# A two-layer graph kernel on one core: the features' bias and relu leave GpSimd, b2 is added ahead of the strips, and the row gathers are cut into other lots

## The chip, the cores and the metric

One core of one Trainium2 chip. The metric is the device time of one execution in microseconds (us). The engines are called PE (TensorE, the matmuls), DVE (VectorE), ACT (ScalarE), POOL (GpSimd) and SP (SyncE, which here only issues transfers).

## The reference

```
h = relu(layernorm(x));  x = x + L0(h, adj)
h = relu(layernorm(x));  x = x + L1(h, adj)

L0:  tanh(concat[h, t] @ W1 + b1) @ W2 + b2
     + adj @ (h @ B.T) - rowsum(adj) * (h @ B.T)
L1:  feats = h @ W                      (8 heads of 8)
     scores = leaky_relu(a_self[i] + a_neigh[j]) - 1e10 * (1 - adj[i, j])
     relu(softmax(scores) @ feats + bias)
```

x is 8192 x 64 and adj is 8192 x 8192, both float32, so adj is 256 MB. adj holds values from 0 to 1, not zeros and ones, so the term of -1e10 leaves for each row only the neighbour with the largest adj. The second layer's output for row i is therefore relu(feats[best[i]] + bias), with best[i] the column of the largest value of row i. The kernel checks at its end that this shortcut held and has a general path behind a branch, which does not run here.

## The kernel before, in words

**Strips and chunks.** The 8192 rows are 16 strips of 512 rows (S = 16), a strip is four tiles of 128 rows (TB = 4), 64 tiles in all. Of each strip adj arrives transposed in 8 chunks of 2 MB. SP loads them into a ring of four slots (`load`); a slot is loaded again when PE (`pe_chunk`) and DVE (`hi_done`) have both used it.

**PE**, for each strip: `sums` and `products` of the 8 chunks (row sums and adj @ h). Between them stand the small steps of the strip before: `turn_maxima(s-1)`, which waits for DVE's `runmax_done`; `turn_sums(s-1)`, `turn_h1(s-1)`, `features(s-1)`; and at the end `mlp_hidden(s)`.

**DVE**, for each strip: `fold_chunk` takes the running maximum over the chunks (two operations of 128x2048 each), `fold_maxima` folds it down to `runmax` (L623, L625, L628). Between chunks 3 and 4 stand `search_classes(s-1)`, which finds for each row the class of columns that holds the maximum (`cls_row`, L646), and `residual(s-1)` with the second layernorm; `search_candidates(s-1)` after chunk 6 gives `best`.

**ACT** copies PE's results out of PSUM (`finish_strip`), with the tanh, the square root and the copy of `feats` (L541).

**POOL** is one queue in program order. For each strip: `add_b2(s)` (L393: x_tq + b2, 128x256), `store_agg(s-1)` (L400: feats + bias; L404: maximum with 0; L406: a store of 128 KB to `agg_dram`, and a wait until it has landed), `fetch_candidates(s)` (L413: four indirect transfers). From strip 11 on it also gathers `agg_dram[best]` (L420: one indirect transfer for a tile of 128 rows). Strips 0 to 14 are gathered in five lots, by the table `WINDOWS = (known, s0, s1)`: once agg is stored for strips below `known`, strips s0 to s1 are gathered. The rows of which `best` lies in a strip that was not yet stored are mended at the end: up to 8 for each partition (`SLOTS`), gathered again by L453 and added to the output by L463. The last strip's four tiles are gathered with these.

**The head.** Strip 0 runs while DVE and ACT normalise x (`centre`, `normalise`: L602 is the last operation of each eighth, `pro_norm`). PE's `products` of chunk c waits for `pro_norm` c+1. `constants()` (L567 to L577) stands on DVE before the last chunk's fold; PE's first `mlp_hidden` waits for it. `x_tq` is loaded by SP behind the chunks of strip 0, and POOL's first `add_b2` waits for that load.

**The tail.** After PE has finished strip 15, DVE works out `best` for the last strip, `add_x1` (L764) adds the residual to the gathered rows, SP stores them, and POOL issues what is left of its queue.

Of the kernel before, what the change touches and what calls it, by code (L numbers as in the profile page):

```python
# [23 lines left out]
ALU = mybir.AluOpType  # L24
# [12 lines left out]
CB = 8  # L37
# [11 lines left out]
SPAN = 8192  # L49
WINDOWS = ((11, 0, 3), (12, 3, 6), (13, 6, 9), (14, 9, 12), (15, 12, 15))  # L50
EARLY = 12 * TB
LATE = 15 * TB


def build(nc, x, adj, adj_t, w1, w1_t, b1, t_in, w2, b2, b_t, w_gat, w_gat_t, att_self, att_neigh, bias, out):
    with ExitStack() as ctx:
        def sb(name, shape, dt=F32):
            return ctx.enter_context(nc.sbuf_tensor(name, shape, dt))
# [4 lines left out]
        def sem(name):  # L63
            return ctx.enter_context(nc.semaphore(name))
# [60 lines left out]
        good = sb("good", [P, 6])  # L125
        agg = sb("agg", [P, TB * D])
        agg_last = sb("agg_last", [P, TB, D])
        is_late = sb("is_late", [P, LATE])
# [64 lines left out]
        zero_stored = sem("zero_stored")  # L193
        agg_chain = sem("agg_chain")
        agg_stored = sem("agg_stored")
# [27 lines left out]
        dve_past = sem("dve_past")  # L223
        pe_past = sem("pe_past")

        gen_turned = sem("gen_turned")
# [111 lines left out]
        def _(pool):  # L338
# [51 lines left out]

            def add_b2(s):
                x1 = x_tq[:, bass.ds(s * TB, TB), :]
                pool.tensor_tensor(x1, x1, b2_row[:, :].unsqueeze(1).to_broadcast([P, TB, D]),  # L393
                                   ALU.add).then_inc(x_b2_done, 1)

            def store_agg(s):

                pool.wait_ge(feat_done, s + 1)
                a = feats_v[:, bass.ds(s * TB, TB), 0:D]
                pool.tensor_tensor(agg[:, :].rearrange("q (k d) -> q k d", d=D), a,  # L400
                                   bias_row[:, :].unsqueeze(1).to_broadcast([P, TB, D]), ALU.add).then_inc(agg_chain, 1)
                pool.wait_ge(agg_chain, s * 2 + 1)
                pool.sem_inc(pool_past, 1)
                pool.tensor_scalar(agg[:, :], agg[:, :], 0.0, None, ALU.max).then_inc(agg_chain, 1)  # L404
                pool.wait_ge(agg_chain, s * 2 + 2)
                pool.dma_start(agg_by_q[:, bass.ds(s, 1), :].rearrange("q a f -> q (a f)"), agg[:, :]).then_inc(agg_stored, 16)  # L406
                pool.wait_ge(agg_stored, s * 16 + 16)

# [15 lines left out]

            def round_(s):
                add_b2(s)
                store_agg(s - 1)
                fetch_candidates(s)

            add_b2(0)  # L430
            fetch_candidates(0)
            n0 = WINDOWS[0][0]
            with pool.Fori(1, n0) as s:
                round_(s)
            for w, (known, s0, s1) in enumerate(WINDOWS):
                add_b2(known)
                if w:
                    pool.wait_ge(got[w - 1], 16 * TB * (WINDOWS[w - 1][2] - WINDOWS[w - 1][1]))
                store_agg(known - 1)
                pool.wait_ge(best_done, s1)  # L440
                if known < S - 1:
                    gather(w, s0 * TB, s0 * TB + TB)
                    fetch_candidates(known)
                    gather(w, s0 * TB + TB, s1 * TB)
                else:
                    gather(w, s0 * TB, s1 * TB)
                    fetch_candidates(known)

# [29 lines left out]
        def _(act):  # L478
# [42 lines left out]

            def finish_strip(s, last=False):

# [22 lines left out]
            act.wait_ge(dve_const, 4)  # L546
            with act.Fori(0, S - 1) as s:
                finish_strip(s)
# [12 lines left out]
        def _(dve):  # L561
# [104 lines left out]
            def residual(s):  # L666
# [8 lines left out]
                dve.wait_ge(chain, c0 + 2)  # L675
                dve.wait_ge(x_b2_done, s + 1)
                dve.tensor_tensor(x1, x1, tmp[:, :, :], ALU.add).then_inc(x1_done, 1)
# [17 lines left out]

            def strip(s):

                dve.wait_ge(runmax_done, s)
                for c in range(NC):
                    fold_chunk(s, c)  # L700
                    if c == 3:
                        search_classes(s - 1)
                        residual(s - 1)
                    if c == 4:
                        scale_h1(s - 1)
                    if c == 6:
# [15 lines left out]
            fold_maxima(0)  # L722
            with dve.Fori(1, S) as s:
                strip(s)
            search_classes(S - 1)
            residual(S - 1)
# [337 lines left out]
```

## Time and profile before

| what | value |
|---|---|
| median of 3 runs | 844.42 us (842.97 to 845.2) |
| the profiled execution | 846.39 us, its span 844.7 us |
| PE, DVE, POOL, ACT busy | 767.9, 732.3, 316.0, 130.0 us |
| PE's granted clock, mean | 0.96 of full |
| transfers | 282.80 MB, mean 335 GB/s over the span |

Busy time is the time in which an engine executes; the span runs from the first to the last instruction. A granted clock of 1.00 is 2.4 GHz, and 0.50 is 1.2 GHz. A DVE or POOL duration includes the time that the instruction waited for its operands' path into SBUF, so an operation of one shape can show different durations.

### The profile page before, as it was taken

The numbers are of one execution on the slowest core, as the hardware profiler recorded it, in microseconds if no ns is written. First come the engines' busy times: TensorE is split into PE (matmuls) and PEld (weight loads), VectorE is DVE, ScalarE is ACT, GpSimd is POOL, SyncE is SP. The second block draws the span as 40 slices with busy tenths as digits, with TensorE's granted clock in tenths as the row PEclk, the third lists the DMA queues.
The fourth block names the chain that finished last, engine by engine and source line by source line (L and its number), as shares of the span: only waits on it lengthen the run. The fifth ranks groups of instructions, "written<-read, shape, count | busy, mean of one in ns | idle before, by whom it ended". The sixth has DMA issues, their size and how long they took to land.

```text
span 844.7 us, 13444 instructions
## 1 busy us (share of the span) xinstructions
PE 767.9 (91%) x5222; PEld 275.6 (33%) x5222; DVE 732.3 (87%) x963; ACT 130.0 (15%) x212; POOL 316.0 (37%) x247
## 2 busy tenths in 40 slices
PE   4998999999999999999999999999999999999100
PEld 1333333333434343333334343333334343433100
DVE  4899998999998989989898999989898999999420
ACT  2344011020202011110202020111102020111100
POOL 7000312212131313111131313131586868778775
PEclk9998999999999999999999999999999999999655
DMA  8997898999898998989898998989998999983152
GB/s 331 419 401 287 316 380 331 396 368 386 324 388 343 370 379 334 380 355 399 337 383 328 388 379 332 377 336 383 371 385 348 390 359 374 397 335 137 26 124 21
DMA packets 30190, 282.80 MB, mean 335 GB/s; under 512 B 6176, under 2 KB 10640, under 8 KB 13664
## 3 DMA queue, kind: packets, MB, share of 16 engines
q1 hardware_dynamic: 23168, 275.00, 81.1%
q0 software_dynamic: 7008, 7.63, 3.8%
q8 instruction: 7, 0.11, 0.1%
q14 instruction: 7, 0.06, 0.0%
HBM read 277.37 MB, written 5.24 MB: 335 GB/s over the span
## 4 chain that ended last, share of the span: by engine, by line
PE 67%; POOL 18%; DMA 9%; issue 4%; DVE 1%; ACT 0%; SPq 0%; POOLq 0%; DVEq 0%; ACTq 0%
PE acc L869 39%; PE row_sums L877 20%; POOL gathered L420 10%; DMA ring<-in_adj_t 4%; POOL cand L413 3%; DMA gathered<-agg_dram,best 2%; DMA agg_dram<-agg 2%; PE ps_hid L884 1%; POOL out L463 1%; POOL agg L404 1%; POOL agg L400 1%; PE ps_feat L926 1%; PE ps_xb L905 1%; PE ps_acc L898 1%; POOL max_hi L453 1%
## 5 line engine op out<-in xcount | busy, mean ns | idle before, releaser
L869 PE MATMUL acc<-ring,x_pb 128*64 128x512 f32 x2048 | 449.7, 596 | 0.0
L877 PE MATMUL row_sums<-ring,ones_cols 128*32 128x512 f32 x2048 | 235.0, 604 | 13.0 <-DMA ring<-in_adj_t 13.0
L616 DVE TENSOR_TENSOR max_lo<-max_lo,ring 128x2048 f32<-128x2048 f32 x96 | 220.6, 2298 | 28.2 <-DMA ring<-in_adj_t 27.5
L869 PEld LDWEIGHTS acc<-ring,x_pb 128*64 128x64 f32 x2048 | 144.2, 137 | 283.9 <-issue 280.6
L617 DVE TENSOR_TENSOR max_hi<-max_hi,ring 128x2048 f32<-128x2048 f32 x96 | 219.2, 2283 | 0.0
L413 POOL DMA_INDIRECT cand<-in_adj,cls_row x64 | 83.7, 1308 | 225.8 <-DVE cls_row L646 210.0
L420 POOL DMA_INDIRECT gathered<-agg_dram,best x64 | 110.2, 1722 | 40.3 <-DMA agg_dram<-agg 22.3
L877 PEld LDWEIGHTS row_sums<-ring,ones_cols 128*32 128x32 f32 x2048 | 61.7, 111 | 158.8 <-issue 156.5
L400 POOL TENSOR_TENSOR agg<-feats,bias_row 128x256 f32<-128x256 f32 x15 | 24.7, 1648 | 192.8 <-ACT feats L541 187.9
L393 POOL TENSOR_TENSOR x_tq<-x_tq,b_row 128x256 f32 (+1 forms) x16 | 26.1, 1634 | 42.6 <-DMA x_tq<-in_x 42.2
L541 ACT COPY feats<-ps_feat 128x320 f32 (+1 forms) x16 | 6.8, 427 | 218.5 <-PE ps_feat L926 216.5
L623 DVE TENSOR_TENSOR max_lo<-max_lo,max_hi 128x2048 f32<-128x2048 f32 x16 | 36.7, 2293 | 2.0
L611 DVE TENSOR_TENSOR max_lo<-ring 128x2048 f32<-128x2048 f32 x16 | 36.7, 2292 | 2.0
L613 DVE TENSOR_TENSOR max_hi<-ring 128x2048 f32<-128x2048 f32 x16 | 38.2, 2386 | 0.0
L534 ACT ACTIVATE stat<-stat,eps 128x4 f32<-128x4 f32 x16 | 4.8, 298 | 184.8 <-DVE stat L688 184.8
L404 POOL TENSOR_SCALAR agg<-agg 128x256 f32<-128x256 f32 x15 | 26.3, 1754 | 3.0 <-POOL agg L400 3.0
L625 DVE TENSOR_TENSOR max_lo<-max_lo 128x1024 f32<-128x1024 f32 x16 | 24.6, 1535 | 0.5
L655 DVE MAX8 top_cand<-cand 128x8 f32<-128x64 f32 x64 | 9.6, 212 | 14.5 <-DMA cand<-in_adj,cls_row 14.5
L990 PE MATMUL ps_hid<-ones,good 128*1 128x1 f32 x2 | 0.2, 164 | 23.9 <-DVE good L792 23.9
L884 PE MATMUL ps_hid<-h_strip,w_sb 128*128 128x256 f32 x64 | 19.0, 421 | 2.9 <-ACT h_strip L519 2.9
L534 ACT ACT_TABLE_LOAD x16 | 20.5, 1283 | 0.3
L513 ACT ACT_TABLE_LOAD x16 | 20.5, 1283 | 0.3
(130 smaller groups left out, 481.8 us busy)
## 6 DMA issues: line engine op xcount, KB each, us to landing
ring<-in_adj_t SPq DMA_DIRECT2D x128, 2048.0 KB, 8.7
agg_dram<-agg POOLq DMA_DIRECT2D x20, 128.0 KB, 6.9
x_tq<-in_x SPq DMA_DIRECT2D x1, 2048.0 KB, 14.0
x_pb<-in_x SPq DMA_DIRECT2D x1, 1536.0 KB, 14.6
out<-gathered SPq DMA_DIRECT2D x1, 1536.0 KB
cand<-in_adj,cls_row POOLq DMA_INDIRECT x64
gathered<-agg_dram,best POOLq DMA_INDIRECT x64, 6.2
x_pb<-in_x SPq DMA_DIRECT2D x1, 512.0 KB, 4.6
```

The costliest lines, as they stand in the source:

```text
L400: pool.tensor_tensor(agg[:, :].rearrange("q (k d) -> q k d", d=D), a, bias_row[:, :].unsqueeze(1).to_broadcast([P, TB, D]), ALU.add).then_ ...
L404: pool.tensor_scalar(agg[:, :], agg[:, :], 0.0, None, ALU.max).then_inc(agg_chain, 1)
L413: pool.indirect_dma_start(out=cand[:, k, :], out_offset=None, in_=classes, in_offset=bass.IndirectOffsetOnAxis(ap=cls_row[:, k:k + 1], axi ...
L420: pool.indirect_dma_start(out=gathered[:, t, :], out_offset=None, in_=agg_dram, in_offset=bass.IndirectOffsetOnAxis(ap=best[:, t:t + 1], a ...
L611: dve.tensor_tensor(max_lo[:, :], lo, hi, ALU.max).then_inc(hi_done, 1)
L613: dve.tensor_tensor(max_hi[:, :], lo, hi, ALU.max).then_inc(hi_done, 1)
L616: dve.tensor_tensor(max_lo[:, :], max_lo[:, :], lo, ALU.max).then_inc(lo_done, 1)
L617: dve.tensor_tensor(max_hi[:, :], max_hi[:, :], hi, ALU.max).then_inc(hi_done, 1)
L623: dve.tensor_tensor(max_lo[:, :], max_lo[:, :], max_hi[:, :], ALU.max).then_inc(fold, 1)
L869: last = pe.matmul(acc[0][at:at + D, :], x_pb[:, c * CB + b, :], slot(c)[:, b * W:(b + 1) * W], start=(c == 0 and b < 2), stop=(c == NC - ...
L877: last = pe.matmul(row_sums[at:at + QUAD, :], ones_cols[:, :], slot(c)[:, b * W:(b + 1) * W], start=(c == 0 and b < 4), stop=(c == NC - 1 ...
L884: last = pe.matmul(ps_hid[:, k * (W // 2):(k + 1) * (W // 2)], w1_sb[:, k * HID:(k + 1) * HID], h_strip[:, :], start=True, stop=True)
```

## The change

POOL's two arithmetic operations for each strip leave it. DVE adds the bias (`add_bias(s-2)`, behind the first fold of strip s, into a new buffer `agg_pre`), ACT takes the relu (`rectify(s-1)`, behind the tanh in `finish_strip`), and POOL only issues the store, whose landing is now awaited before the gathers and no longer right behind the store. The 16 additions of b2, one for each strip, become four of 128x1024 ahead of strip 0's candidates; `residual` waits for all four. The lots change from 12, 12, 12, 12, 12 tiles to 8, 16, 16, 16 and 4; the candidates are fetched ahead of the gathers, but for the last strip behind them. `EARLY`, the rows that the first large `add_x1` takes, goes from 48 to 56 tiles.

```diff
-WINDOWS = ((11, 0, 3), (12, 3, 6), (13, 6, 9), (14, 9, 12), (15, 12, 15))
-EARLY = 12 * TB
+WINDOWS = ((11, 0, 2), (12, 2, 6), (13, 6, 10), (14, 10, 14), (15, 14, 15))
+EARLY = 14 * TB
...
-            def add_b2(s):
-                x1 = x_tq[:, bass.ds(s * TB, TB), :]
-                pool.tensor_tensor(x1, x1, b2_row[:, :].unsqueeze(1).to_broadcast([P, TB, D]),
+            def add_b2(g):
+                x1 = x_tq[:, g * CB * 2:(g + 1) * CB * 2, :]
+                pool.tensor_tensor(x1, x1, b2_row[:, :].unsqueeze(1).to_broadcast([P, CB * 2, D]),
                                    ALU.add).then_inc(x_b2_done, 1)
 
             def store_agg(s):
 
-                pool.wait_ge(feat_done, s + 1)
-                a = feats_v[:, bass.ds(s * TB, TB), 0:D]
-                pool.tensor_tensor(agg[:, :].rearrange("q (k d) -> q k d", d=D), a,
-                                   bias_row[:, :].unsqueeze(1).to_broadcast([P, TB, D]), ALU.add).then_inc(agg_chain, 1)
-                pool.wait_ge(agg_chain, s * 2 + 1)
-                pool.sem_inc(pool_past, 1)
-                pool.tensor_scalar(agg[:, :], agg[:, :], 0.0, None, ALU.max).then_inc(agg_chain, 1)
-                pool.wait_ge(agg_chain, s * 2 + 2)
+                pool.wait_ge(agg_ready, s + 1)
                 pool.dma_start(agg_by_q[:, bass.ds(s, 1), :].rearrange("q a f -> q (a f)"), agg[:, :]).then_inc(agg_stored, 16)
-                pool.wait_ge(agg_stored, s * 16 + 16)
...
-            add_b2(0)
+            for g in range(NB // (2 * CB)):
+                add_b2(g)
             fetch_candidates(0)
...
             for w, (known, s0, s1) in enumerate(WINDOWS):
-                add_b2(known)
                 if w:
                     pool.wait_ge(got[w - 1], 16 * TB * (WINDOWS[w - 1][2] - WINDOWS[w - 1][1]))
                 store_agg(known - 1)
+                if known < S - 1:
+                    fetch_candidates(known)
+                pool.wait_ge(agg_stored, 16 * known)
                 pool.wait_ge(best_done, s1)
...
+                gather(w, s0 * TB, s1 * TB)
+            fetch_candidates(S - 1)
...
+            def rectify(s, first):
+                if first:
+                    act.wait_ge(zero_stored, 16 * (S - WINDOWS[0][0]))
+                else:
+                    act.wait_ge(agg_stored, s * 16)
+                act.sem_inc(act_past, 1)
+                act.wait_ge(agg_pre_ready, s + 1)
+                act.activation(agg[:, :], agg_pre[:, :], ACT.Relu).then_inc(agg_ready, 1)
...
                 tanh(s)
+                if behind:
+                    rectify(s - 1, behind == 1)
                 act.wait_ge(acc_turned, s + 1)
...
-                dve.wait_ge(x_b2_done, s + 1)
+                dve.wait_ge(x_b2_done, NB // (2 * CB))
...
+            def add_bias(s):
+
+                dve.wait_ge(feat_done, s + 1)
+                dve.tensor_tensor(agg_pre[:, :].rearrange("q (k d) -> q k d", d=D), feats_v[:, bass.ds(s * TB, TB), 0:D],
+                                  bias_row[:, :].unsqueeze(1).to_broadcast([P, TB, D]), ALU.add).then_inc(agg_pre_ready, 1)
...
                 for c in range(NC):
                     fold_chunk(s, c)
+                    if c == 0 and not first:
+                        add_bias(s - 2)
...
+            add_bias(S - 2)
             search_classes(S - 1)
```

POOL's queue before, from the last zero store through the loop's body over strips 1 to 10 (line numbers are those of each kernel; ISA and REGISTER_ALU rows are waits and their bookkeeping):

```order
L384 DMA agg_dram<-agg 128x256 x5
L393 TENSOR_TENSOR x_tq<-x_tq,b_row 128x256
L413 DMA cand<-in_adj,cls_row 128x64 x4
L433 UNCONDITIONAL_BRANCH
L433 ISA
L393 TENSOR_TENSOR x_tq<-x_tq,b_row 128x256
L400 ISA
L400 TENSOR_TENSOR agg<-feats,bias_row 128x256
L402 ISA
L404 TENSOR_SCALAR agg<-agg 128x256
```

The same place now:

```order
L387 DMA agg_dram<-agg 128x256 x5
L396 TENSOR_TENSOR x_tq<-x_tq,b_row 128x1024 x4
L408 DMA cand<-in_adj,cls_row 128x64 x4
L424 UNCONDITIONAL_BRANCH
L402 ISA
L402 DMA agg_dram<-agg 128x256
L405 REGISTER_ALU
L408 DMA cand<-in_adj,cls_row 128x64 x4
```

Four additions, each of four times the width, now stand ahead of the first candidates, and the loop's body holds no arithmetic.

POOL's queue before, from the gathers of the lot `known = 14` to the first mending gathers:

```order
L406 DMA agg_dram<-agg 128x256
L420 DMA gathered<-agg_dram,best 128x64 x4
L413 DMA cand<-in_adj,cls_row 128x64 x4
L420 DMA gathered<-agg_dram,best 128x64 x8
L393 TENSOR_TENSOR x_tq<-x_tq,b_row 128x256
L400 TENSOR_TENSOR agg<-feats,bias_row 128x256
L404 TENSOR_SCALAR agg<-agg 128x256
L406 DMA agg_dram<-agg 128x256
L420 DMA gathered<-agg_dram,best 128x64 x12
L413 DMA cand<-in_adj,cls_row 128x64 x4
L453 DMA max_hi<-agg_dram,late_from 128x64 x8
```

The same place now:

```order
L402 DMA agg_dram<-agg 128x256
L408 DMA cand<-in_adj,cls_row 128x64 x4
L415 DMA gathered<-agg_dram,best 128x64 x16
L402 DMA agg_dram<-agg 128x256
L415 DMA gathered<-agg_dram,best 128x64 x4
L408 DMA cand<-in_adj,cls_row 128x64 x4
L442 DMA max_hi<-agg_dram,late_from 128x64 x8
```

Sixteen gathers stand ahead of the last store and four behind it, where twelve and twelve stood (four of the first twelve ahead of the candidates), and three arithmetic operations between them are gone.

DVE's program now, at the start of the body of strips 2 to 15:

```order
L613 TENSOR_TENSOR max_lo<-ring 128x2048
L700 REGISTER_ALU
L701 ISA
L701 TENSOR_TENSOR agg_pre<-feats,bias_row 128x256
L615 TENSOR_TENSOR max_hi<-ring 128x2048
```

The addition of 128x256 in the middle is the new one; the two folds around it are as before.

## Rows read from the trace of the kernel before

**Rows 1.** The page: busy time, granted clock by slices, the chain that ended last.

```profile
PE 767.9 (91%) x5222; PEld 275.6 (33%) x5222; DVE 732.3 (87%) x963; ACT 130.0 (15%) x212; POOL 316.0 (37%) x247
...
PEclk9998999999999999999999999999999999999655
...
PE 67%; POOL 18%; DMA 9%; issue 4%; DVE 1%; ACT 0%; SPq 0%; POOLq 0%; DVEq 0%; ACTq 0%
```

**Rows 2.** Windows: length, busy time of PE, PEld, DVE, ACT, POOL; clock, DMA share, GB/s.

```profile
262.80:309.71 46.91, 46.91 (x324) 16.78 (x323) 43.72 (x56) 6.61 (x12) 10.36 (x8) 1.00 0.90 363
731.08:778.05 46.97, 46.97 (x324) 16.82 (x324) 43.85 (x56) 6.63 (x12) 35.80 (x20) 1.00 0.71 280
```

**Rows 3.** The waits: engine, line, what for: us in all, times, longest.

```profile
DVE max_lo L616 <- DMA ring<-in_adj_t: 27.5, 30, 2.4
```

**Rows 4.** Timeline of the head: start, us, instruction [idle before <-releaser].

```profile
59.56 0.74 POOL L393 TENSOR_TENSOR x_tq<-x_tq,b_row 128x256 f32<-128x256 f32 x1 [42.24 <-DMA x_tq<-in_x]
...
60.92 0.69 DVE L602 SCALAR_TENSOR_TENSOR x_pb<-x_pb,pstat 128x512 f32<-128x512 f32 x1
...
66.65 0.20 DVE L577 COPY fold_rows<-pstat 128x64 f32<-128x64 f32 x1
...
74.86 0.69 DVE L628 TENSOR_TENSOR runmax<-max_lo 128x512 f32<-128x512 f32 x1
...
72.01 2.05 PE L884 MATMUL ps_hid<-h_strip,w_sb 128*128 128x256 f32 x4 [2.92 <-ACT h_strip L519]
...
79.45 0.66 PE L912 MATMUL ps_turn<-ident,runmax 128*128 128x128 f32 x4
```

**Rows 5.** Timeline: operations of POOL and DVE that meet, in strips 1 and 2.

```profile
100.37 2.98 DVE L616 TENSOR_TENSOR max_lo<-max_lo,ring 128x2048 f32<-128x2048 f32 x1 [0.22 <-DMA ring<-in_adj_t]
...
100.44 0.74 POOL L393 TENSOR_TENSOR x_tq<-x_tq,b_row 128x256 f32 x1
...
165.18 2.29 DVE L623 TENSOR_TENSOR max_lo<-max_lo,max_hi 128x2048 f32<-128x2048 f32 x1
165.90 2.16 POOL L400 TENSOR_TENSOR agg<-feats,bias_row 128x256 f32<-128x256 f32 x1 [16.35 <-ACT feats L541]
167.51 1.64 DVE L625 TENSOR_TENSOR max_lo<-max_lo 128x1024 f32<-128x1024 f32 x1
```

**Rows 6.** Timeline: the same of DVE, L625 with no POOL operation beside it, and L613.

```profile
73.60 1.23 DVE L625 TENSOR_TENSOR max_lo<-max_lo 128x1024 f32<-128x1024 f32 x1
...
733.43 2.82 DVE L613 TENSOR_TENSOR max_hi<-ring 128x2048 f32<-128x2048 f32 x1
```

**Rows 7.** Timeline of POOL: its smallest operation that reads and writes SBUF.

```profile
3.56 0.19 POOL L352 TENSOR_SCALAR_AFFINE_SELECT head_mask<-head_mask 64x8 f32<-64x8 f32 x1
```

**Rows 8.** Timeline of POOL from strip 15's candidates to the end.

```profile
750.74 0.95 POOL L413 DMA_INDIRECT cand<-in_adj,cls_row  x1 [0.30 <-issue]
...
774.36 2.12 POOL L420 DMA_INDIRECT gathered<-agg_dram,best  x1 [0.30 <-issue]
776.50 1.00 POOL L393 TENSOR_TENSOR x_tq<-x_tq,b_row 128x256 f32<-128x256 f32 x1
778.08 0.73 POOL L400 TENSOR_TENSOR agg<-feats,bias_row 128x256 f32<-128x256 f32 x1 [0.58 <-DMA gathered<-agg_dram,best]
...
780.16 0.64 POOL L406 DMA_DIRECT2D agg_dram<-agg  x1 [0.30 <-POOL agg L404]
782.51 1.03 POOL L420 DMA_INDIRECT gathered<-agg_dram,best  x1 [1.71 <-DMA agg_dram<-agg]
...
791.62 3.89 POOL L420 DMA_INDIRECT gathered<-agg_dram,best  x1 [0.30 <-issue]
...
804.63 0.96 POOL L413 DMA_INDIRECT cand<-in_adj,cls_row  x1 [0.30 <-issue]
```

**Rows 9.** Timeline of DVE at the end: the last fold and the first large addition.

```profile
776.95 1.10 DVE L628 TENSOR_TENSOR runmax<-max_lo 128x512 f32<-128x512 f32 x1
...
791.35 3.34 DVE L764 TENSOR_TENSOR gathered<-gathered,x_tq 128x3072 f32<-128x3072 f32 x1
```

More of the change, by code:

```diff
@@ L126, in build @@
         agg = sb("agg", [P, TB * D])
+        agg_pre = sb("agg_pre", [P, TB * D])
         agg_last = sb("agg_last", [P, TB, D])
@@ L193, in build @@
         zero_stored = sem("zero_stored")
-        agg_chain = sem("agg_chain")
+        agg_pre_ready = sem("agg_pre_ready")
+        agg_ready = sem("agg_ready")
         agg_stored = sem("agg_stored")
@@ L224, in build @@
         pe_past = sem("pe_past")
+        act_past = sem("act_past")
         gen_turned = sem("gen_turned")
@@ L423, in gather @@
                     ).then_inc(got[w], 16)
[L425 to L428, printed above, removed]
-            add_b2(0)
+            for g in range(NB // (2 * CB)):
+                add_b2(g)
             fetch_candidates(0)
@@ L433, in _ @@
             with pool.Fori(1, n0) as s:
-                round_(s)
+                store_agg(s - 1)
+                fetch_candidates(s)
             for w, (known, s0, s1) in enumerate(WINDOWS):
-                add_b2(known)
                 if w:
@@ L439, in _ @@
                 store_agg(known - 1)
+                if known < S - 1:
+                    fetch_candidates(known)
+                pool.wait_ge(agg_stored, 16 * known)
                 pool.wait_ge(best_done, s1)
[L441 to L447, printed above, removed]
+                gather(w, s0 * TB, s1 * TB)
+            fetch_candidates(S - 1)
             pool.wait_ge(agg_last_stored, 16)
@@ L520, in strip_h, with finish_strip @@
                              h_by_k[:, 2 * k:2 * k + 2, bass.ds(s * P, P)]).then_inc(strip_h_done, 1)
-            def finish_strip(s, last=False):
+            def rectify(s, first):
[6 more added lines that the diff above has]
+                act.activation(agg[:, :], agg_pre[:, :], ACT.Relu).then_inc(agg_ready, 1)
+            def finish_strip(s, last=False, behind=2):
                 act.wait_ge(acc_full, s + 1)
@@ L546, in _ @@
             act.wait_ge(dve_const, 4)
-            with act.Fori(0, S - 1) as s:
+            finish_strip(0, behind=0)
+            finish_strip(1, behind=1)
+            with act.Fori(2, S - 1) as s:
                 finish_strip(s)
@@ L694, in scale_h1, with strip @@
                 dve.tensor_tensor(h1[:, :, :], cen[:, :, :], wide(rstd[:, :], TB), ALU.mult).then_inc(h1_done, 1)
-            def strip(s):
+            def add_bias(s):
+                dve.wait_ge(feat_done, s + 1)
+                dve.tensor_tensor(agg_pre[:, :].rearrange("q (k d) -> q k d", d=D), feats_v[:, bass.ds(s * TB, TB), 0:D],
+                                  bias_row[:, :].unsqueeze(1).to_broadcast([P, TB, D]), ALU.add).then_inc(agg_pre_ready, 1)
+            def strip(s, first=False):
                 dve.wait_ge(runmax_done, s)
@@ L722, in _ @@
             fold_maxima(0)
-            with dve.Fori(1, S) as s:
+            strip(1, first=True)
+            with dve.Fori(2, S) as s:
                 strip(s)
+            add_bias(S - 2)
             search_classes(S - 1)
```

## The prediction

> **What bounds the kernel now.** I read the page first: PE is busy 91% of the span, DVE 87%, POOL only 37%, but the chain that ended last holds 67% of PE and 18% of POOL, and the clock's last slices are low [rows 1]. So there are two stages: strips in which PE is the chain, and a tail in which something on POOL is. The windows say it sharply: in a middle strip PE is busy 46.91 of 46.91 us at a clock of 1.00, DVE 43.72, and the strip in which POOL works 35.80 us takes the same 46.97 [rows 2]. Nothing that takes work off POOL or DVE there can shorten a strip. DVE has spare time: it waited 27.5 us for chunks in 30 waits over the run [rows 3].
>
> The tail is POOL's queue. It issues the candidates of strip 14 from 750.74, and from 774.36 on one thing follows the other with no gap but for landings, to the last candidate of strip 15 at 804.63; the mending gathers, their scatters and the last store stand behind that and take the rest of the 844.7 us [rows 8]. DVE's last fold ends already at 778.05 [rows 9].
>
> The head is a third stage. POOL's first addition of b2 starts at 59.56, when x_tq has landed. DVE ends runmax of strip 0 at 75.55 (74.86 + 0.69) and PE uses it at 79.45, behind its own work [rows 4]: 3.9 us of slack, of which I leave 0.15 to the semaphore, so 3.75.
>
> **The change part by part.**
>
> *Bias on DVE, relu on ACT: nothing.* One addition of 128x256 costs DVE 0.4 us a strip, at a place that is followed by the waits for chunks 2 and 3; those 27.5 us over 15 strips are 1.8 a strip and cover it [rows 3]. DVE also gets back what POOL's operations took from it, below. If that cover were gone, the cost would be 14 x 0.4 = 5.6 us. ACT is busy 6.6 us in a strip of 47 [rows 2]; the copy of acc_tq is queued behind the relu, and DVE's residual waits for that copy, but `add_bias` needs only fold 0 of the strip (2.3 us), and PE's small steps come later than that.
>
> *The 15 relus, 15 bias additions and 15 of 16 additions of b2 that leave POOL's strips.* They ran under PE. They are worth something only in the tail: the last three.
>
> *Four additions of 128x1024 in the head.* This is the expensive part. What a POOL operation does to DVE is to be seen in the two places where they meet. At 100.44 POOL adds 256 columns in 0.74 us, and the fold of 2048 columns that started 0.07 before takes 2.98 instead of 2.29: 0.69 lost. At 165.90 POOL has to wait (2.16 instead of 0.74), gets its turn when the fold L623 ends at 167.47, and L625 behind it takes 1.64 [rows 5] instead of 1.23; L613 at 733.43 takes 2.82 instead of 2.29 [rows 6]. So they exclude each other, POOL gets its turn at the next boundary of DVE's two-input operations, and 256 columns cost DVE 0.41, 0.53 or 0.69 us. The head had one such addition, and it was over before L602 began [rows 4].
>
> The width now is four times. How long is 1024 columns? No row shows one. The smallest POOL operation takes 0.19 [rows 7]; if that is the fixed part, 0.55 us is for 256 columns and 1024 take 0.19 + 4 x 0.55 = 2.39. Then the first runs from 59.56 to 61.95 and holds DVE's L602 (start 60.92) by 1.0. The other three are queued, each gets its turn behind one DVE operation (L602, L616, L617), and each holds the next one by four times 0.41 to 0.69, that is 1.6 to 2.8; I take 2.0. Together runmax of strip 0 is 1.0 + 3 x 2.0 = 7.0 us later. PE absorbs 3.75 of it, so PE is late by 7.0 - 3.75 = 3.2 us. `mlp_hidden(0)` waits for fold_rows too, which moves from 66.85 to 73.9, past its old start of 72.01 by 1.9 [rows 4]; that is less than 3.2 and lies in it. PE has no gap later in which to win it back, so it stays to the end: **+3.2**. Bounds: if only half of an add's cost scales with its width, the first holds nothing and the queued ones 1.6 each, 4.8, so +1.1; if everything scales, 4 x 0.74 = 2.96 for the first (1.6 held) and 2.8 for each of the others, 10.0, so +6.3.
>
> The Trainium skill's GPSIMD Engine Reference (3.1, Elementwise) gives 4.5 us for such an addition of 2048 columns; between that and 0.74 here, 1024 would be 2.35 by estimate, close to 2.39. The skill's SBUF page ("SBUF — State Buffer", SBUF: two separate sides) says that whichever starts first keeps the shared port pair "for the whole instruction"; taken at its word with 2.35 for all four, DVE would be late by about 8.1 and PE by 4.3. The rows at 100.44 agree with the rule and those of the queued operation show less. No row here shows a wide one.
>
> DVE itself is late by 7.0 and PE by 3.2 going into strip 1. The slots of the ring that DVE frees late (chunks 6 and 7 of strip 0) carry chunks 2 and 3 of strip 1, which PE needs only after some 12 us of other work. DVE then gains on PE by its spare 1 to 3 us a strip, so I cost this at nothing.
>
> *The lots and the tail.* POOL is free at strip 14's candidates in both kernels. From 750.74 to 776.48 it issues 12 items (four candidates, eight gathers), at 2.1 us each, because under DVE's folds an issue waits for their boundaries [rows 8]. Now 8 of 16 gathers are left at 776.8: one under DVE's last fold (2.2), seven at 1.26 (the pace behind 782.51), so to 787.5. The landing of the last takes 1.6 (776.48 to 778.08), the store's 2.35 (780.16 to 782.51) [rows 8]: four gathers start at 791.5. The large `add_x1` starts then on DVE: it took 3.34 us for 3072 columns and stretched one gather to 3.89 [rows 8, 9]; 3584 columns make 3.9 and about 4.4. So the four end at 799.7, and four candidates at 1.26 each end at 804.7, against 805.6. That is 0.9 won; if one more gather fits before 776.48, since the candidates no longer stand behind four gathers, it is 2.1. I take **-1.5**. Bounds: 0 when a landing takes 1 us more, and -4.5 if `add_x1` falls into the wait for the store instead of on a gather. It is this little since the number of issues in the chain is the same (28); the lot of four only moves eight gathers ahead of the store, and what is truly gone are the three POOL operations, 776.50 to 780.16 less a landing of 1.6.
>
> Sum: +3.2 - 1.5 = +1.7 us. The profiled execution took 846.39 (span 844.7), so it would be 848.1; the median of the runs is 0.2% lower, 844.42, and becomes **846.1**.
>
> **The rivals.**
>
> *The head is hidden, the tail gains (faster).* If the additions hold DVE by less than 3.75 us altogether, PE never sees them. That decides it: under 0.9 for each of four. For it: 0.41 at 256 columns may be mostly a handover that doesn't grow. Against: 0.69 of 0.74 was lost at 100.44. Then the time is 844.4 less 1.5 to 4.5: 840 to 843, say 842.
>
> *The additions hold DVE for their whole length at four times 0.74 (slower).* PE late by 6.3, 844.4 + 6.3 - 1.5 = 849.2. For it: the unqueued row. Against: both queued rows show less. It decides for "slower" as soon as DVE loses over 7.8 us.
>
> *The lots of 16 don't fit under a strip.* Twenty issues at 2.1 are 42 us, with the landings and the store 46 of 46.9. If POOL falls behind, candidates come late, and each us is added at strip 15: some 3 us, 849. DVE's small operations, where an issue takes 1.26, speak against it.
>
> *It doesn't do what it says:* it would have to keep POOL's arithmetic in the strips or leave the mending list too short; the order shows that the first is gone, and the second would let the general path run, whose operations this trace lacks.
>
> **How the numbers follow.** The forecast has 0.48, with its own range 843.5 to 848; the hidden head 0.28; the full hold 0.16; the lots that don't fit 0.08. What a measurement here can tell from no change is 0.3%, 2.5 us, so 841.9 to 846.9 is "same". The forecast's case lies in it for four fifths, else above; the hidden head is faster in three of four. Faster 0.21, same 0.45, slower 0.34. The range leaves out 1 in 10 on each side: 841.0 to 849.5.
>
> **What would show it.** POOL's four additions from 59.56, 2.4 us or more each; DVE's L602, L616, L617 around 61 to 73 stretched by 2; runmax of strip 0 at about 82.5 and PE's first turn of it at 82.7 for 79.45; strips of 46.9 after that; POOL's last candidate at 804.7 plus 3.2. Wrong would be: a PE that turns the maxima at 79.5, a tail shorter by more than 4 us, or a strip that is no longer full of PE.

## The result and the profile after

The changed kernel takes 853.87 us (median of 5 runs, 853.54 to 855.06) against 844.42 before (842.97 to 848.17): a ratio of 1.011, 95% interval 1.0083 to 1.0136. The forecast was 846.1 in a range that ended at 849.5. The profiled execution took 853.87, its span 852.1.

The page after, to be held against [rows 1]: busy time, granted clock, the chain that ended last.

```profile
PE 766.7 (90%) x5222; PEld 275.4 (32%) x5222; DVE 732.2 (86%) x978; ACT 135.9 (16%) x227; POOL 254.5 (30%) x205
...
PEclk9998999999999999999999999999999999999655
...
PE 64%; POOL 16%; DVE 8%; issue 6%; DMA 4%; POOLq 0%; ACT 0%; SPq 0%; DVEq 0%
```

POOL lost 61.5 us of work, ACT has 5.9 us more (the relu), the others have as much as before, and yet the span is 7.4 us longer. What is new is DVE with 8% of the chain. The windows say that it isn't in the middle; the same stretches as in [rows 2]:

```profile
262.80:309.71 46.91, 46.91 (x324) 16.73 (x322) 43.21 (x57) 6.93 (x12) 5.55 (x5) 1.00 0.91 364
731.08:778.05 46.97, 46.97 (x326) 16.73 (x322) 42.45 (x57) 6.94 (x12) 35.67 (x20) 1.00 0.82 316
```

PE is as full as before at the same clock. From PE's turn of h in strip 1 to its last group of products it is 656.38 us, before 656.41. So the loss is ahead of that and behind it.

**The head after**, timeline (start, us, instruction, idle time before and its releaser), for [rows 4]:

```profile
60.30 13.85 POOL L396 TENSOR_TENSOR x_tq<-x_tq,b_row 128x1024 f32<-128x1024 f32 x4 [42.98 <-DMA x_tq<-in_x]
...
60.59 2.61 DVE L604 SCALAR_TENSOR_TENSOR x_pb<-x_pb,pstat 128x512 f32<-128x512 f32 x1
63.12 4.45 DVE L618 TENSOR_TENSOR max_lo<-max_lo,ring 128x2048 f32<-128x2048 f32 x1
67.50 4.45 DVE L619 TENSOR_TENSOR max_hi<-max_hi,ring 128x2048 f32<-128x2048 f32 x1
71.87 2.43 DVE L569 TENSOR_SCALAR att_diag<-head_mask,att_col 64x8 f32<-64x8 f32 x2
...
82.88 0.69 DVE L630 TENSOR_TENSOR runmax<-max_lo 128x512 f32<-128x512 f32 x1
...
63.34 3.65 PE L881 MATMUL acc<-ring,x_pb 128*64 128x512 f32 x16 [1.31 <-DVE x_pb L604]
74.36 0.40 PE L989 MATMUL ps_feat<-att_diag,w_gat_t_sb 64*64 64x16 f32 x4 [4.51 <-DVE hid_bias L571]
76.16 2.05 PE L896 MATMUL ps_hid<-h_strip,w_sb 128*128 128x256 f32 x4 [1.40 <-ACT h_strip L508]
83.62 0.66 PE L924 MATMUL ps_turn<-ident,runmax 128*128 128x128 f32 x4 [1.21 <-DVE runmax L630]
108.21 0.41 PE L931 MATMUL ps_turn<-ident,h 128*128 128x128 f32 x2 [0.86 <-DVE h L696]
```

Each of the four additions holds one stretch of DVE: L604 by 1.9 us (2.61 for 0.69), two folds by 2.16 each (4.45 for 2.29), att_diag by 2.1 (2.43 for 0.35). runmax of strip 0 ends at 83.57 for 75.55, 8.0 later, and PE turns it at 83.62 for 79.45, 4.2 later. Then comes a wait that the forecast hadn't: PE waits 0.86 us for h of strip 1, at 108.21.

**The tail after**, for [rows 8, 9]:

```profile
661.46 0.97 POOL L408 DMA_INDIRECT cand<-in_adj,cls_row  x1 [14.54 <-DVE cls_row L648]
...
701.33 3.05 POOL L415 DMA_INDIRECT gathered<-agg_dram,best  x1 [0.30 <-issue]
710.01 0.59 POOL L402 DMA_DIRECT2D agg_dram<-agg  x1 [5.62 <-DMA gathered<-agg_dram,best]
...
760.34 0.59 POOL L402 DMA_DIRECT2D agg_dram<-agg  x1 [5.82 <-DMA gathered<-agg_dram,best]
761.23 2.48 POOL L408 DMA_INDIRECT cand<-in_adj,cls_row  x1 [0.30 <-issue]
...
797.32 0.59 POOL L402 DMA_DIRECT2D agg_dram<-agg  x1 [1.78 <-DMA gathered<-agg_dram,best]
799.61 0.97 POOL L415 DMA_INDIRECT gathered<-agg_dram,best  x1 [1.69 <-DMA agg_dram<-agg]
...
806.22 4.49 POOL L408 DMA_INDIRECT cand<-in_adj,cls_row  x1 [0.31 <-issue]
...
812.27 0.95 POOL L408 DMA_INDIRECT cand<-in_adj,cls_row  x1 [0.30 <-issue]
...
785.41 0.41 ACT L518 ACTIVATE agg<-agg_pre 128x256 f32<-128x256 f32 x1
797.69 0.38 ACT L530 COPY acc_tq<-ps_acc 128x260 f32<-128x260 f32 x1 [11.88 <-remote]
...
806.00 3.88 DVE L776 TENSOR_TENSOR gathered<-gathered,x_tq 128x3584 f32<-128x3584 f32 x1
```

POOL starts strip 12's candidates on time (it had waited 14.54 us). Its 20 issues end at 704.38, 42.9 us later. Then it stands 5.62 us for the landing of the lot: 48.6 us from those candidates to the store at 710.01, a strip having 46.9. The next such stretch takes 50.3. In the table below, strip 14's first candidate is so 5.4 us later against PE than before. And ACT stands still for 11.88 us ahead of its copy of acc_tq, which pushes DVE's large add_x1 to 806.00. There it falls on a candidate, whose issue takes 4.49 us; before, it fell on a gather, which took 3.89 [rows 8].

To compare kernels I count from marks of the same trace. In the head: PE's turn of the eighth part of x (61.37 before, 60.97 after) as zero. In the tail: the start of PE's last group of products (759.53 and 764.59) as zero. All in us; the names are explained above.

| | runmax turned | h of strip 1 turned | strip 14's first candidate | large add_x1 | last candidate ends |
|---|---|---|---|---|---|
| before | 18.1 | 41.8 | -8.8 | 31.8 | 46.1 |
| after | 22.7 | 47.2 | -3.4 | 41.4 | 48.6 |
| e5 after again | 22.9 | 47.5 | -3.3 | 41.4 | 48.6 |
| e1 head only | 22.8 | 47.5 | -9.0 | 31.7 | 44.6 |
| e7 16 x 256 in head | 20.1 | 46.0 | -3.1 | 41.4 | 48.6 |
| e2 b2 spread | 17.1 | 40.7 | -2.7 | 32.5 | 46.1 |
| e8 before, b2 spread | 15.3 | 39.0 | -8.8 | 31.7 | 46.0 |
| e4 bias and relu only | 16.9 | 40.6 | -9.1 | 31.7 | 47.2 |
| e3 old lots | 22.7 | 47.3 | -9.0 | 31.8 | 47.3 |
| e6 b2 spread, lots 12 12 16 16 4 | 17.3 | 40.9 | -6.2 | 39.6 | 46.9 |
| e9 b2 spread, covered landings | 16.9 | 40.6 | -9.0 | 31.8 | 44.1 |
| e10 after, covered landings | 22.8 | 47.4 | -9.0 | 31.8 | 44.1 |

### The profile page after: what moved, and what is told of

Read it like the earlier page. It is cut to its first block, busy times and chain, and to the rows that moved or that the text cites. A ratio compares the mean times of both kernels' runs of the same rounds, so it can differ in the third digit from the quotient of the medians.

```text
span 852.1 us, 13399 instructions
## 1 busy us (share of the span) xinstructions
PE 766.7 (90%) x5222; PEld 275.4 (32%) x5222; DVE 732.2 (86%) x978; ACT 135.9 (16%) x227; POOL 254.5 (30%) x205
## 4 chain that ended last, share of the span: by engine, by line
PE 64%; POOL 16%; DVE 8%; issue 6%; DMA 4%; POOLq 0%; ACT 0%; SPq 0%; DVEq 0%
PE acc L881 38%; PE row_sums L889 19%; POOL gathered L415 10%; DMA ring<-in_adj_t 4%; POOL cand L408 3%; DVE max_hi L619 3%; DVE max_lo L618 2%; PE ps_hid L896 1%; POOL out L452 1%; PE ps_feat L938 1%; PE ps_xb L917 1%; PE ps_acc L910 1%; POOL max_hi L442 1%; PE ps_turn L924 1%; PE ps_acc L915 1%
## 5 line engine op out<-in xcount | busy, mean ns | idle before, releaser
L408 POOL DMA_INDIRECT cand<-in_adj,cls_row x64 | 90.7, 1418 | 218.2 <-DVE cls_row L648 202.7
L415 POOL DMA_INDIRECT gathered<-agg_dram,best x64 | 105.7, 1651 | 20.9 <-issue 18.6
L402 POOL DMA_DIRECT2D agg_dram<-agg x15 | 8.9, 592 | 299.8 <-ACT agg L518 286.6
L625 DVE TENSOR_TENSOR max_lo<-max_lo,max_hi 128x2048 f32<-128x2048 f32 x16 | 36.7, 2292 | 2.0
L613 DVE TENSOR_TENSOR max_lo<-ring 128x2048 f32<-128x2048 f32 x16 | 36.7, 2291 | 1.9
L396 POOL TENSOR_TENSOR x_tq<-x_tq,b_row 128x1024 f32<-128x1024 f32 x4 | 13.8, 3490 | 43.0 <-DMA x_tq<-in_x 43.0
L537 ACT ACTIVATE h_t<-ps_turn 128x256 f32<-128x256 f32 x15 | 5.8, 384 | 90.6 <-PE ps_turn L931 90.6
L627 DVE TENSOR_TENSOR max_lo<-max_lo 128x1024 f32<-128x1024 f32 x16 | 19.6, 1225 | 0.5
L530 ACT COPY acc_tq<-ps_acc 128x260 f32<-128x260 f32 x16 | 6.0, 375 | 77.7 <-PE ps_xb L917 65.8
L776 DVE TENSOR_TENSOR gathered<-gathered,x_tq 128x256 f32<-128x256 f32 (+1 forms) x3 | 4.7, 1575 | 15.8 <-DMA gathered<-agg_dram,best 15.8
## 6 DMA issues: line engine op xcount, KB each, us to landing
agg_dram<-agg POOLq DMA_DIRECT2D x20, 128.0 KB, 20.1
```

Source lines behind the costliest of these rows:

```text
L408: pool.indirect_dma_start(out=cand[:, k, :], out_offset=None, in_=classes, in_offset=bass.IndirectOffsetOnAxis(ap=cls_row[:, k:k + 1], axi ...
L415: pool.indirect_dma_start(out=gathered[:, t, :], out_offset=None, in_=agg_dram, in_offset=bass.IndirectOffsetOnAxis(ap=best[:, t:t + 1], a ...
L613: dve.tensor_tensor(max_lo[:, :], lo, hi, ALU.max).then_inc(hi_done, 1)
L625: dve.tensor_tensor(max_lo[:, :], max_lo[:, :], max_hi[:, :], ALU.max).then_inc(fold, 1)
```

## The experiments

**e1, the four additions alone.** The kernel before, with its 16 additions replaced by the four in the head.

```diff
...
-            add_b2(0)
+            for g in range(NB // (2 * CB)):
+                add_b2(g)
...
-                dve.wait_ge(x_b2_done, s + 1)
+                dve.wait_ge(x_b2_done, NB // (2 * CB))
```

> The kernel before with one part of the change: the four additions of b2 of 128x1024 in the head, and none in the strips. Theory (the head stalls PE for good, and the lots cost the rest): PE's first matmul of strip 1 moves from 82.2 to about 87.3 us and stays 5 us late to the end; POOL's tail loses its addition of 1.0 us ahead of the last store, so +4 to +5 us against the kernel before, a ratio of 1.005 to 1.006. Rival (the loss of the changed kernel comes from the bias on DVE and the relu on ACT, and PE wins the head back): within 1.5 us of the kernel before.

Measured: 850.5 us, ratio 1.0069 (1.005 to 1.0089). The table shows the head of the changed kernel, so the additions alone make it. Its timeline shows who is held:

```profile
59.70 13.20 POOL L393 TENSOR_TENSOR x_tq<-x_tq,b_row 128x1024 f32<-128x1024 f32 x4 [42.38 <-DMA x_tq<-in_x]
...
59.45 2.29 DVE L615 TENSOR_TENSOR max_lo<-max_lo,ring 128x2048 f32<-128x2048 f32 x1
61.65 4.46 DVE L616 TENSOR_TENSOR max_hi<-max_hi,ring 128x2048 f32<-128x2048 f32 x1
66.03 4.60 DVE L566 TENSOR_SCALAR att_diag<-head_mask,att_col 64x8 f32<-64x8 f32 x2
...
70.73 2.20 DVE L571 TENSOR_TENSOR hid_bias<-hid_bias 128x1 f32<-128x1 f32 x1
```

In this execution DVE was further on: L604's counterpart had ended at 59.53, so POOL's first addition, released at 59.70, was queued behind a fold that had begun. All four additions then hold something: the next fold by 2.17, the two small operations of 64x8 by 2.1 each (4.60 for 0.35) and one of 128x1 by 2.04. Whatever DVE does next pays. PE waits for h of strip 1 (0.94 us) and once more for h of strip 2 (1.06 us), so here DVE's lateness outlives strip 1.

**e2, b2 in pieces.** The changed kernel with b2 as eight additions of 128x512, one in the head and one in each of strips 1 to 7.

```diff
-                x1 = x_tq[:, g * CB * 2:(g + 1) * CB * 2, :]
+                x1 = x_tq[:, bass.ds(g * CB, CB), :]
...
+            with pool.Fori(1, NB // CB) as s:
+                add_b2(s)
+                store_agg(s - 1)
+                fetch_candidates(s)
...
```

> The changed kernel with the additions of b2 taken out of the head: eight of 128x512, one ahead of strip 0's candidates and one in each of strips 1 to 7. Theory: the head's stall of PE is gone, PE's first products of strip 1 at about 82.5 us, and the rest of the loss (POOL late at strip 14's candidates) stays: +2.5 us against the kernel before (ratio 1.003), 7 us less at the last pieces than the changed kernel is over before. Rival (the loss is in bias, relu or lots alone): +8 us or more stays, ratio 1.009.

Measured: 844.65 us, ratio 0.9996 (0.9983 to 1.0009). The whole loss is gone, more than expected (a ratio of 1.003), for the tail came out better too. POOL is as late as in the changed kernel (-2.7), but ACT doesn't stand still:

```profile
59.92 1.27 POOL L396 TENSOR_TENSOR x_tq<-x_tq,b_row 128x512 f32<-128x512 f32 x1 [42.56 <-DMA x_tq<-in_x]
...
781.49 0.38 ACT L533 COPY acc_tq<-ps_acc 128x260 f32<-128x260 f32 x1 [2.14 <-PE ps_xb L920]
...
790.64 3.89 DVE L779 TENSOR_TENSOR gathered<-gathered,x_tq 128x3584 f32<-128x3584 f32 x1 [0.69 <-DMA gathered<-agg_dram,best]
793.09 2.29 POOL L415 DMA_INDIRECT gathered<-agg_dram,best  x1 [1.69 <-DMA agg_dram<-agg]
```

add_x1 lies mostly in the wait for the store, and the gather behind it takes 2.29 where a candidate took 4.49. Of the profiles here it is the only one in which add_x1 meets that wait; elsewhere it lengthens an issue to 3.3 to 4.5 us. So the 46.1 of e2 is in part a lucky meeting: its last store starts 32.7 us behind the start of the last products, as late as in the changed kernel.

**e3, the lots of before.** The changed kernel with the old table.

```diff
-WINDOWS = ((11, 0, 2), (12, 2, 6), (13, 6, 10), (14, 10, 14), (15, 14, 15))
-EARLY = 14 * TB
+WINDOWS = ((11, 0, 3), (12, 3, 6), (13, 6, 9), (14, 9, 12), (15, 12, 15))
+EARLY = 12 * TB
```

> The changed kernel with the lots of the kernel before (five of 12 tiles), in the new order (candidates ahead of the gathers). Theory: POOL is not behind at strip 14's candidates any more (first of them within 1 us of DVE's cls_row), but the chain behind them has 4+12+12+4 = 32 issues for 28, so 4 x 1.26 = 5 us more of issuing against 5.4 us less of lateness: the same time as the changed kernel within 2.5 us, +8 to +11 us against before. Rival (the large last but one lot itself is the loss, not the lateness): 4 us or more faster than the changed kernel.

Measured: 851.26 us, ratio 1.0093 (1.0074 to 1.0112). With 16 issues a strip POOL is on time (-9.0), and the last candidate comes at 47.3. So the large lots are a loss of 1.3 us against the old ones in this program, although the old ones leave four more issues for the end, and the head remains.

**e4, bias and relu alone** moved in the kernel before (the `add_bias` and `rectify` of the diff).

```diff
...
-                pool.wait_ge(feat_done, s + 1)
...
+                pool.wait_ge(agg_ready, s + 1)
...
```

> The kernel before with one part of the change: the bias added on DVE and the relu taken on ACT, while b2, lots and order of the gathers stay. Theory: PE's strips stay at 46.9 us; POOL loses two operations and their gaps ahead of the last store (1.9 us), so -1 to -2.5 us against before (ratio 0.997 to 0.999). Rival (the moved work costs: the copy of acc_tq waits behind the relu, DVE is late with each strip): slower than before by 2 us or more, with PE late by a few tenths in each strip.

Measured: 844.71 us, ratio 1.0004 (0.9987 to 1.0022). None of the 1 to 2.5 us that were expected, and the timeline of its tail says why:

```profile
772.40 2.17 POOL L396 TENSOR_TENSOR x_tq<-x_tq,b_row 128x256 f32<-128x256 f32 x1
779.48 0.60 POOL L402 DMA_DIRECT2D agg_dram<-agg  x1 [4.91 <-ACT agg L525]
```

The store waits 4.91 us for the relu, which stands behind ACT's tanh. POOL's two operations went, a wait for ACT took their place.

**e5, the changed kernel again.**

> The changed kernel once more, unaltered. In its first profile ACT stood still for 11.9 us ahead of the last copy of acc_tq, and the large addition on DVE then started at 806.0 and held one of POOL's candidate issues (4.49 us). Theory (the standstill belongs to this program and costs the 2.5 us that the tail is longer than in e2_spread_b2): it is there again, the last candidate ends 48.6 us behind the start of PE's last products, and the time is 9 us over before. Rival (a matter of that one execution): ACT waits 2 us there, the last candidate ends about 46 us behind that start, and the median of the runs has another part that is not explained yet.

Measured: 852.68 us, ratio 1.0095 (1.007 to 1.012). ACT's standstill is there again (11.81 us, the copy at 796.31), so it isn't an accident of one execution.

**e6, the lots 12, 12, 16, 16, 4** on e2.

```diff
-WINDOWS = ((11, 0, 2), (12, 2, 6), (13, 6, 10), (14, 10, 14), (15, 14, 15))
+WINDOWS = ((11, 0, 3), (12, 3, 6), (13, 6, 10), (14, 10, 14), (15, 14, 15))
```

> e2_spread_b2 with lots of 12, 12, 16, 16 and 4 tiles instead of 8, 16, 16, 16 and 4: one lot of 16 less ahead of strip 14's candidates. Theory (every lot of 16 with its landing takes POOL 2.5 to 3.5 us more than the 46.9 of a strip): POOL is late by one such step less, the first candidate of strip 14 comes 2.5 to 3.5 us earlier against PE, and the time is 2 to 3 us under e2_spread_b2, a ratio of 0.996 to 0.998 against before. Rival (DVE's pace in the last strip sets the tail, not the start): same as e2_spread_b2.

Measured: 844.72 us, ratio 1.0001 (0.9984 to 1.0018). The 2 to 3 us that were expected below e2 don't show. POOL is less late (-6.2, and its last store 1.7 us earlier than in e2), but ACT stands still (10.09 us) and add_x1 falls on a candidate (4.48 us), so that the stretch from that store to the last candidate is 2.5 us longer.

**e7, the same columns in the head as 16 additions of 128x256.**

```diff
-                x1 = x_tq[:, g * CB * 2:(g + 1) * CB * 2, :]
+                x1 = x_tq[:, g * TB:(g + 1) * TB, :]
...
```

> The changed kernel with the same sum of b2 in the head cut into 16 additions of 128x256 instead of four of 128x1024. Theory (POOL gets a turn at each boundary of DVE's two-input operations and holds the next by 0.45 us for 256 columns): about nine turns up to runmax of strip 0, 4 us, which PE's slack nearly covers, and 16 turns, 7 us, at the second handover (h1), where PE has 3: PE late by about 4 us to the end instead of 5.5, so 1 to 2 us under the changed kernel. Rival (the hold is per operation whatever its width): 16 holds of 2 us, far slower than the changed kernel. Rival (DVE yields only when it is idle): no stall, 5 us under the changed kernel.

Measured: 852.82 us, ratio 1.0096 (1.0072 to 1.0121). Timeline of its head:

```profile
59.81 27.23 POOL L396 TENSOR_TENSOR x_tq<-x_tq,b_row 128x256 f32<-128x256 f32 x16 [42.44 <-DMA x_tq<-in_x]
...
61.70 2.81 DVE L618 TENSOR_TENSOR max_lo<-max_lo,ring 128x2048 f32<-128x2048 f32 x1
64.43 2.81 DVE L619 TENSOR_TENSOR max_hi<-max_hi,ring 128x2048 f32<-128x2048 f32 x1
...
81.04 0.66 PE L924 MATMUL ps_turn<-ident,runmax 128*128 128x128 f32 x4 [3.03 <-DVE runmax L630]
106.93 0.64 PE L931 MATMUL ps_turn<-ident,h 128*128 128x128 f32 x2 [2.16 <-DVE h L696]
107.50 15.37 PE L881 MATMUL acc<-ring,x_pb 128*64 128x512 f32 x64
```

A queued addition of 256 columns holds a fold by 0.52 us, one of 1024 by 2.16, about four times: the hold goes by columns, not by instructions. By runmax less is lost (20.1 for 22.7), since only part of the 16 are through; more is collected at the turn of h (2.16 us of wait). Even so h is turned 1.2 us earlier than in the changed kernel, and the time is the same. Most of that gain is lost right behind the turn: the 64 products there take 15.37 us, the next 64 take 13.95, and PE's granted clock is 0.88 from 107.5 to 120 us. So the 1 to 2 us that were expected below the changed kernel don't show.

**e8, the kernel before with b2 spread as in e2** (the same diff, on the kernel before).

> The kernel before with b2 added in eight operations of 128x512, one in the head and one in each of strips 1 to 7, and none in the last strips; bias, relu, lots and order as before. Theory: POOL's tail loses the addition ahead of the last store, as in e1_head_only where the last candidate ended 1.4 us earlier against PE, and PE's strips stay full: ratio 0.998 to 0.999, -1 to -1.5 us. Rival (512 columns in a strip hold DVE by 1.1 us and PE feels it): 0 or slower.

Measured: 844.95 us, ratio 1.0008 (0.9991 to 1.0025). Taking the additions out of strips 8 to 15, and so out of the tail, gives nothing that can be measured; 1 to 1.5 us were expected.

**e9 and e10, covered landings.** POOL's stretches from strip 11 on in another order: two candidates, landing of the lot before, store, two candidates, landing of the store, gathers. e9 is that on e2, e10 on the changed kernel.

```diff
+                if known < S - 1:
+                    fetch_candidates(known, half=1)
                 if w:
                     pool.wait_ge(got[w - 1], 16 * TB * (WINDOWS[w - 1][2] - WINDOWS[w - 1][1]))
                 store_agg(known - 1)
                 if known < S - 1:
-                    fetch_candidates(known)
+                    fetch_candidates(known, half=2)
                 pool.wait_ge(agg_stored, 16 * known)
```

> The change with b2 spread over the first eight strips (as in the spread run), and POOL's stretches from strip 11 on written in another order: two candidates, the wait for the landing of the lot before, the store of agg, the other two candidates, the wait for the store, the gathers. Nothing of the computation is left out. Theory (POOL falls behind under the strips because the two landings, 5.7 and 2 us, stand bare on top of 20 issues): the landings are now covered by candidates, POOL keeps strip pace, strip 14's candidates start 9 us ahead of PE's last products as before the change (2.7 us ahead in the spread run), and as only 16 + 4 + 4 issues follow, the last candidate ends at +40 to +43 after the start of the last products (46.07 in the spread run): 839 to 842 us, ratio 0.994 to 0.998. Rival 1 (POOL's pace under DVE's folds is the limit, the landings are hidden in it anyway): candidates of strip 14 still start within 4 us of the last products, 844 to 845. Rival 2 (ACT stands still until POOL is done, or the large add_x1 falls on the issues): strip 14's candidates are early, but the last one ends at 44 or later, 842.5 to 844.5.

> The change exactly as made, with its four additions of 128x1024 in the head, and only POOL's stretches from strip 11 on in the other order (two candidates, landing, store, two candidates, store's landing, gathers). Nothing of the computation is left out. Theory (head and tail are two separate losses that add): the head keeps its loss of 5.5 to 6.5 us (runmax of strip 0 turned 22.7 after PE's turn of the eighth part, the middle 656.4 long), the tail gains what the run with b2 spread gains by the same reordering, so this kernel stands 5.5 to 8 us above that one: 846 to 849, ratio 1.002 to 1.006. Rival (POOL's lateness of the head reaches the tail, so that the reordering does nothing): 852 to 854, ratio 1.009 to 1.011.

Measured: e9 843.21 us, ratio 0.9989 (0.9972 to 1.0005); e10 849.27 us, ratio 1.0058 (1.0042 to 1.0074). Timeline of PE, POOL and ACT in e10:

```profile
154.93 0.41 PE L934 MATMUL ps_turn<-ident,h 128*128 128x128 f32 x2 [1.58 <-DVE h L699]
...
709.92 0.95 POOL L409 DMA_INDIRECT cand<-in_adj,cls_row  x1 [0.30 <-issue]
712.16 0.59 POOL L402 DMA_DIRECT2D agg_dram<-agg  x1 [1.29 <-DMA gathered<-agg_dram,best]
...
755.48 0.95 POOL L409 DMA_INDIRECT cand<-in_adj,cls_row  x1 [2.40 <-DVE cls_row L651]
...
787.81 0.38 ACT L533 COPY acc_tq<-ps_acc 128x260 f32<-128x260 f32 x1 [2.14 <-PE ps_xb L920]
...
797.12 3.88 POOL L416 DMA_INDIRECT gathered<-agg_dram,best  x1 [0.30 <-issue]
```

POOL waits for DVE again (2.40) instead of being behind, strip 14's candidates start at -9.0, ACT doesn't stand still, and the last candidate ends at 44.1 in both, 4.5 us earlier than in the changed kernel. The head of e10 keeps its loss, and PE waits 1.58 us more for h of strip 2. So head and tail are two losses that add. For e9, 839 to 842 us and a last candidate at 40 to 43 were expected. It ends at 44.1, because add_x1 still lengthens a gather there (3.94 us; 3.88 in e10), as its second rival had said. e9 has the lowest median of all, but its interval takes in no change: I can't call it faster than the kernel before.

## Why the prediction was wrong

**The sum, term by term.** Head: +3.2 forecast, +5.5 measured (41.8 to 47.2 at the turn of h), 2.3 more. Tail: -1.5 forecast, +2.1 measured at the end of POOL's queue (77.6 to 79.7 behind the last products; +2.6 at the last candidate), 3.6 more. And 2.0 us from scaling the profiled execution to the median. Together 7.9 us, the miss being 7.8. The sum closes only nearly: the changed kernel reached the mark of the head 0.4 us earlier, and its end lies 2.3 us further behind the last products, not 2.1.

Two steps failed. The head's loss, forecast at 3.2 us, had its first addition priced too low and its second handover at nothing. The tail's gain rested on a POOL that is free at strip 14's candidates, and it was 5.4 us later there than before.

**The head's mechanism was right, its size too small.** The slack was forecast as 3.75 us and is 3.85 (DVE 8.0 later, PE 4.2). "The first holds 1.0": it held 1.9 here, because it began at 60.30, ahead of DVE's operation by 0.29 us and not by 1.4; where DVE's operation is already over (e1) it is queued and holds the next one in full. When x_tq lands varies from profile to profile: POOL started between 59.47 and 60.45. "The other three 2.0 each" were 2.1. So the step at fault up to here is the small price of the first addition: four additions cost four holds, 8.3 us. From the figure in the Trainium skill's GPSIMD Engine Reference (3.1, Elementwise) and the rule of a whole hold in the Trainium skill's "SBUF — State Buffer" (SBUF: two separate sides) I had estimated 8.1 and 4.3. The trace agrees with these totals (8.0 and 4.2), better than with my own sum, but in part by luck: the estimate was 1.0 for the first and 2.35 for each of the others, and the trace has 1.9 and 2.1 to 2.2.

**"PE has no gap later in which to win it back" was right, "I cost this at nothing" wrong.** The middle is 656.4 us in both. (It isn't in every kernel with a loaded head: 657.5 in e1, 658.0 in e7 and e10, with the wait at strip 2 or the low clock behind the turn of h. Those 1.1 to 1.6 us belong to the head's loss too.) But DVE, 8 us late, was late a second time at the turn of h of strip 1 (+0.9, e7: 2.16). I had named the slots of the ring as DVE's next customer and not the residual, which PE waits for too.

**"POOL is free at strip 14's candidates in both kernels" was wrong.** The rival "lots of 16 don't fit under a strip" was true, and had 0.08. I gave 42 us to the issues, which is right (42.9), and 4 to landings and store. The landing of a lot took 5.62 and 5.82 us there; 1.6, which I had, is that of the tail, where the ring is quiet (1.78 after). The kernel before didn't show this for its lots, only for its stores. In its waits (us in all, times, longest), the first row is the stores, four of five under strips and one of 1.71 in the tail, the second the lots:

```profile
POOL gathered L420 <- DMA agg_dram<-agg: 22.3, 5, 5.7
POOL agg L400 <- DMA gathered<-agg_dram,best: 4.9, 4, 2.0
```

Its lots under strips had landed 4.2, 2.3 and 2.0 us behind the last issue's end, and an addition of b2 covered part of that. Over all profiles this span runs from 2.0 to 6.3 us under the ring's traffic (6.3 in e8, with lots of 12), so the size of the lot doesn't set it; what does is open.

e9 and e10 show the term: with landings covered POOL is on time, and the last candidate comes 2.0 us earlier than before the change, where -1.5 was forecast. So the count of issues and the three operations were priced about right, for a POOL that is on time; the order of its queue isn't that of the change, though.

**What the tail lost** against e10, which is the changed kernel on time, is 4.5 us at the last candidate (44.1 to 48.6). It splits at POOL's last store. That starts 29.1 us behind the start of the last products in e10 and 32.7 in the changed kernel: 3.6 us of lateness. From there to the last candidate it is 15.0 us in e10 and 15.9 in the changed kernel: 0.9, most of it add_x1, which lengthens one issue to 3.88 in e10 and to 4.49 in the changed kernel. e2 is as late at that store (32.7), but needs only 13.4 from there on. So ACT's standstill costs 0.9 us against an add_x1 that falls on a gather, and 2.5 against one that falls into the landing.

The standstill is there in after, e5, e6 and e7 and not in e2, e3, e4, e9 and e10. Its cause is open: the trace names no instruction as releaser, the copy starts 0.3 to 0.4 us after POOL's last store issue each time, and ahead of it PE too has stretches of "issue" within its small steps (1.15 us in after, 1.12 twice in e6, none in e2). The queues that load instructions moved nothing between 160 and 800 us in after, e6 and e2, so a fetch of code doesn't show as the cause. Lateness of POOL alone doesn't bring it, since e2 is late and free of it.

**Bias and relu at nothing** was right in the strips, which stay 46.9 us long; and in e4 they gave nothing in the tail either.

**The median.** The kernel before is 0.2% faster at its median than in its profile; the changed one isn't. The windows of PE's clock in the gap of the head (length, PE, PEld, DVE, ACT, POOL busy, clock, DMA share, GB/s), of the kernel before:

```profile
68.00:72.00 4.00, 1.08 (x12) 0.81 (x11) 3.96 (x3) 3.00 (x7) 0.00 (x0) 0.88 0.98 393
72.00:76.00 4.00, 3.99 (x16) 1.75 (x20) 3.79 (x4) 2.93 (x4) 0.00 (x0) 0.50 1.01 385
76.00:80.00 4.00, 4.00 (x28) 1.05 (x20) 4.00 (x2) 0.00 (x0) 0.00 (x0) 0.77 0.69 287
```

Of e8, whose head waits the same way:

```profile
72.00:76.00 4.00, 3.79 (x32) 1.62 (x36) 3.79 (x4) 3.10 (x5) 0.00 (x0) 1.00 0.94 352
```

Of the changed kernel:

```profile
72.00:76.00 4.00, 0.40 (x4) 0.29 (x4) 3.93 (x7) 1.12 (x4) 2.15 (x1) 0.58 0.74 213
76.00:80.00 4.00, 3.84 (x16) 1.69 (x20) 3.96 (x3) 3.06 (x5) 0.00 (x0) 0.57 0.75 317
```

PE idles about 3 us in the gap, and the clock falls to 0.50 (1.2 GHz) in the profile of before and stays at 1.00 (2.4 GHz) in e8, 2.8 us apart at the turn of h (41.8 and 39.0). e2, e4, e6 and e9, with the same gap, lie between: 0.57 to 0.59 from 72 to 76 us and 0.99 or 1.00 behind, and h turned at 40.6 to 40.9. In the changed kernel, where PE waits longer, the clock fell in each of the profiles with four additions in the head. Of the kernel before there is one profile, with the longest fall among those with this gap, so it is likely that other executions of it lose less there. What is on record of them fits: with e5, they ran from 841.64 us at a mean clock of 0.965 to 848.85 at 0.958. On this the fallen clock of the old profile hid 1 to 3 us of the change's price. Where in those executions the clock fell isn't shown, so for the medians this is argued.

## What to carry over

A wide GpSimd operation queued against a busy VectorE is paid by VectorE for its whole width, whatever the small operation it hits: put such work where VectorE has waits, in pieces, or under stages that TensorE bounds. Before adding issues to a queue that runs at a strip's pace, add its bare landing waits as they are under full traffic, with their whole range (2.0 to 6.3 us here), not as they are in a quiet tail, and cover them with issues that don't depend on them. When two kernels are compared by their ends, split the difference at a mark between: e2's tail looked half healed, and its POOL was as late as the changed kernel's. When a late engine is costed, list all its customers of the next stage.

## What was not expected of the hardware

- An addition of 128x1024 on POOL held DVE by 1.9 to 2.2 us, even for operations of 128x1 (2.20 instead of 0.16).
- A lot's last gather landed 2.0 to 4.2 us after its issue under the ring's traffic in the kernel before, 5.6 to 5.8 in the changed one, up to 6.3 in e8, and 1.5 to 1.8 in the quiet tail; what sets it is open.
- ACT stood still for 10.1 to 11.9 us in four profiles, up to 0.3 to 0.4 us after a store issue of POOL; cause open.
- TensorE's clock after one and the same idle gap of about 3 us was 0.50 in one kernel's profile, 0.57 to 0.59 in four others' and 1.00 in another's.
